# One product of two per-row numbers in the input scale's chain, with two scalar operands instead of a second tensor

## The reference, cut to what matters

```python
def bit_linear(x, w, b):
    gamma_x = clip(max(abs(x), axis=-1), 1e-05, None)
    scale_x = 127.0 / gamma_x
    x_dq = clip(round(x * scale_x), -128.0, 127.0) / scale_x
    gamma_w = clip(mean(abs(w)), 1e-05, None)
    w_dq = clip(round(w / gamma_w), -1.0, 1.0) * gamma_w
    return einsum('bsd,hd->bsh', x_dq, w_dq) + b

x = x + L0_xattn(layernorm(x), ctx)                   # stage A
h = silu(bit_linear(xn, gate_w)) * bit_linear(xn, val_w)   # xn = layernorm(x)
x = x + bit_linear(h, out_w)                          # stage B
x = x + L1_xattn(layernorm(x), ctx)                   # stage D
x = x + L1_ffn(layernorm(x))                          # stage C
```

## Time and profile before

| | us |
|---|---|
| three runs, median | 837.59 |
| lowest and highest of them | 830.35, 840.47 |
| the profiled execution | 840.63 |
| its span, from the first to the last instruction | 838.8 |

### The profile page before, as it was taken

The page is one execution under the profiler, slowest core; times in us unless marked ns, Lnnn a source line. Parts: engine busy times, 40 slices in busy tenths (PEclk is TensorE's granted clock), DMA queues, the critical chain, the costliest instruction groups (busy, mean ns, idle before and its releaser), DMA issues. The chain is left out here.

```text
span 838.8 us, 22126 instructions
## 1 busy us (share of the span) xinstructions
PE 763.0 (91%) x6898; PEld 398.9 (48%) x6898; DVE 752.7 (90%) x1636; ACT 701.4 (84%) x1447; POOL 634.2 (76%) x1139
## 2 busy tenths in 40 slices
PE   2677899999999999999999999999999989898886
PEld 1333444454555554555555555555545445444444
DVE  5688899999899999999999999999989989787865
ACT  3888888888799998999989999999979889688644
POOL 3827566788888887888888888888878877677632
PEclk9557899999999999999999999999999999899989
DMA  9401222244443444454544444544443434344230
GB/s 311 133 21 39 59 75 77 65 114 88 94 115 95 115 97 106 109 112 108 113 109 106 112 110 114 115 99 112 109 97 101 104 84 112 72 91 97 57 69 20
DMA packets 197952, 82.59 MB, mean 98 GB/s; under 512 B 139710, under 2 KB 196670, under 8 KB 197836
## 3 DMA queue, kind: packets, MB, share of 16 engines
q1 hardware_dynamic: 193260, 74.63, 38.1%
q10 hardware_dynamic: 4576, 6.55, 2.4%
HBM read 28.15 MB, written 4.69 MB: 39 GB/s over the span
## 5 line engine op out<-in xcount | busy, mean ns | idle before, releaser
L1120 DVE TENSOR_REDUCE mx<-psS 128x2 f32<-128x512 f32 x512 | 333.3, 679 | 21.0 <-PE psS L617 19.9
L799 ACT ACTIVATE prob<-psT 128x512 f32<-128x512 f32 x512 | 292.4, 603 | 23.2 <-PE psT L625 15.4
L617 PE MATMUL psS<-KQ 31*128 31x256 f16 x1024 | 137.7, 284 | 15.1 <-DVE mx L1120 12.1
L639 PE MATMUL psW<-prob,vst 128*32 128x256 f32 x2048 | 143.0, 400 | 0.0
L728 PE MATMUL psW<-guT,xT 128*128 128x512 bf16 x512 | 133.5, 390 | 6.3 <-DMA xT<-stage 5.1
L625 PE MATMUL psT<-KQ 32*128 32x256 f16 x1024 | 129.4, 280 | 3.9 <-ACT prob L799 3.0
L639 PEld LDWEIGHTS psW<-prob,vst 128*32 128x32 f32 x2048 | 55.2, 112 | 61.5 <-issue 34.6
L728 PEld LDWEIGHTS psW<-guT,xT 128*128 128x128 f16 x512 | 43.3, 99 | 72.8 <-issue 38.8
L1004 POOL TENSOR_TENSOR hqB<-wide,rnd 128x512 bf16<-128x512 f32 x60 | 63.4, 1058 | 14.7 <-ACT wide L847 14.4
L617 PEld LDWEIGHTS psS<-KQ 31*128 31x128 f16 x1024 | 40.0, 93 | 72.4 <-DVE mx L1120 46.1
L1018 POOL TENSOR_TENSOR stage<-stage 128x512 f16<-128x512 f32 x60 | 69.6, 1161 | 2.6 <-ACT stage L908 0.5
(11 more groups left out here) (190 smaller groups left out, 1791.0 us busy)
## 6 DMA issues: line engine op xcount, KB each, us to landing
KQ<-hl SPq DMA_DIRECT2D x192, 64.0 KB, 1.9
xP<-in_x SPq DMA_DIRECT2D x32, 128.0 KB, 2.2
cP<-in_ctx SPq DMA_DIRECT2D x32, 128.0 KB, 2.1
xA<-in_x SPq DMA_DIRECT2D x32, 128.0 KB, 2.6
cB<-in_ctx SPq DMA_DIRECT2D x32, 128.0 KB, 2.3
oV<-uA SPq DMA_DIRECT2D x32, 128.0 KB, 2.1
out<-x SPq DMA_DIRECT2D x32, 128.0 KB, 2.1
oR<-rden_d SPq DMA_DIRECT2D x120, 32.0 KB
```

The lines of the kernel that those rows point to most:

```text
L617: m = nc.tensor.matmul(psS[:, n % 2, T * k:T * k + T], KQ[p % DEEP][r, 1, g, 128 * k:128 * k + 128], KQ[p % DEEP][r, 0, g, :], start=True, ...
L639: m = nc.tensor.matmul(bank[32 * j:32 * j + 32, :], vst[p % DEEP][:, k, 4 * n + j, :], prob[:, (4 * n + j) % 8, k, :], start=(k == 0), sto ...
L799: m = nc.scalar.activation(flat(prob[:, n % 8, :, :]), psT[:, n % 2, :], ACT.Exp, scale=float(HC) ** -0.5)
L1120: m = nc.vector.tensor_reduce(mx[:, p % 2, :, 4 * (n % 4) + n // 4], psS[:, n % 2, :].rearrange("p (c s) -> p c s", c=NK), AX.X, ALU.max)
```

## The change

Line 1195 computes (s * s) * g, with s the scale of a row and g a constant of the weights. Before, the first s is a tensor of 128x1, the second s a per-partition scalar, and g a second tensor, all in SBUF. After, the one tensor is s, and the two scalars are s and g. The operations, their order, the destination and the place in the list are the same.

```diff
@@ -1192,8 +1192,7 @@
                     sc = sB[:, p % 2, :]
                     inner(1, nc.vector.tensor_scalar(sc[:, 1:2], sc[:, 0:1], 1e-5, 1.0 / 127.0, ALU.max, ALU.mult))
                     nc.vector.tensor_scalar(sc[:, 4:5], sc[:, 1:2], gam_q[:, 0:1], None, ALU.mult)
-                    nc.vector.scalar_tensor_tensor(out=sc[:, 5:6], in0=sc[:, 1:2], scalar=sc[:, 1:2],
-                                                   in1=gam_q[:, 1:2], op0=ALU.mult, op1=ALU.mult)
+                    nc.vector.tensor_scalar(sc[:, 5:6], sc[:, 1:2], sc[:, 1:2], gam_q[:, 1:2], ALU.mult, ALU.mult)
                     m = nc.vector.reciprocal(sc[:, 2:3], sc[:, 1:2])
```

## The result

The changed kernel took 827.1 us (median of 20 runs, 822.0 to 837.2) against 834.7 us for the kernel before in the same comparison. The ratio is 0.9924, with a 95% interval from 0.9896 to 0.9951: a gain of 6.3 us, from 4.1 to 8.7, clear of zero and well inside two per cent. The profiled execution's span is 828.4 us; before it was 838.8.

The account below looks back on a forecast made before the run. A loop through VectorE and GpSimd, closed by line 1195's hold, was taken to set the pace. Gains of 6.0 us (steady stretch) and 3.1 us (head and tail), rounded to 9, gave 837.6 - 9 = 828.6 us; range 820 to 838.

Parts of the forecast that it names:

- The hold and its cause: Line 1195 on VectorE, with two SBUF tensors, waits for the running GpSimd instruction: 20.8 us for 32, 13.95 us removable.
- The rival that the new form is held likewise: At line 1195 the new form is held like the old; time stays at 837 to 838 us; chance 0.05.
- The price of the new form: New line 1195: 214 ns each, taken from line 1194, so 6.85 us for 32 instructions.
- The loop: Steady stretch: rot's end releases line 1195, VectorE runs to mvC, which releases GpSimd's rsC; 6.86 + 15.06 = 21.92 us.
- The floor: Shortest interval from pair to pair in the steady stretch; VectorE's period after the change put at 21.29 us.
- GpSimd as next in line: Steady stretch: without rsC's 0.57 us wait for mvC, GpSimd's period is 21.37 us, and GpSimd is late next.
- TensorE as a bound at 21.52 us: Steady stretch: TensorE's busy share, 0.981 x 21.94 us, limits the saving per period to 0.42 us; called a soft bound.
- The sum: Whole kernel: 6.0 us from twelve steady periods plus 3.1 us from head and tail, 9.1, rounded to 9 us.
- the half: Head and tail: of 6.25 us of VectorE's time saved there, half, 3.1 us, reaches the end.
- The slower rival: Late qT transpose landings, priced at 5.2 us each; three more make the kernel 6.6 us slower, 844 us; chance 0.06.
- All of it and more: TensorE's bound is soft and the outlier's loss goes too: 14 to 17 us gained, 821 to 824 us; chance 0.17.
- Another loop at the same pace: A loop among ScalarE, TensorE and VectorE only 0.1 us shorter: 1 to 4 us gained, 834 to 837 us; chance 0.17.

Follow-up runs that it names:

- e2: The changed kernel plus one 128x1 product of two SBUF tensors into a scratch tile behind line 1195; 0.9988 of the kernel before.
- e4: The kernel before with the old two-tensor form of line 1195 moved to just ahead of mvC, where GpSimd waits; 0.9930 of the kernel before.
- e8: The changed kernel with three fillers in the new form (one tensor, two per-partition scalars) ahead of line 1195; 832.8 us, run once only.
- e7: The changed kernel with both products (columns 4 and 5) moved from VectorE to GpSimd, behind rq; 0.9977 of the kernel before, 832.8 us.
- e9: The changed kernel itself, unaltered, compared again with the kernel before on another occasion; 0.9951 of the kernel before.
- e3: The kernel before with three 128x1 one-scalar tensor_scalar fillers ahead of the old line 1195; 1.0057 of the kernel before.
- e5: The changed kernel with the reciprocal 1/s ahead of the two products in the same step; 0.9927 of the kernel before, 830.3 us.
- e6: The kernel before with the old line 1195 placed behind the reciprocal, which keeps the signal; 0.9971 of the kernel before, 833.4 us.

## Why the prediction was right, point by point

**The hold and its cause** were right: 128x1 with two tensors from SBUF waits for GpSimd, with one tensor and two per-partition scalars it does not. e2 and e4 show it from both sides. The rival that the new form is held likewise, for which the earlier trace rows spoke, did not come about at this size (that row is taken up below). SBUF — State Buffer of the Trainium skill, section Who interferes with whom, names both the two-input case and the mode of tensor_scalar; the first agrees with e2 (656 ns in the median against 147), and the second does not show at 128x1 (262 to 268 ns in all 32 executions). At 256 elements it may: the earlier trace rows has two executions of one form, and they differ in what GpSimd does meanwhile.

```profile
806.19 1.24 DVE L1134 TENSOR_SCALAR xnC<-x,mvC,rsC 128x256 f32<-128x256 f32 x1
806.12 2.32 POOL L1018 TENSOR_TENSOR stage<-stage 128x512 f16<-128x512 f32 x2
...
822.77 0.41 DVE L1134 TENSOR_SCALAR xnC<-x,mvC,rsC 128x256 f32<-128x256 f32 x1 [0.71 <-POOL rsC L960]
```

The first begins 0.07 us behind a GpSimd instruction and takes 1.24 us; during the second GpSimd runs nothing. All twelve traces have this pair, 1.23 or 1.24 us and 0.41. So the row spoke rightly for a hold at its own size, and the step from 256 elements to one is what failed of that rival. No run varied the size.

**The price of the new form** was mis-sized: 214 ns taken, 265 measured. The group costs 8.5 us instead of 6.85, so 20.8 - 8.5 = 12.3 us of VectorE's time went, not 13.95. What line 1194 could not show is the second per-partition scalar (e8).

**The loop** was right, and so was its removal. The floor was given as 21.29 us by VectorE's sum; with the true price it is 21.94 - (0.86 - 0.265) = 21.35, and 21.36 to 21.37 was measured. The interval from pair to pair was forecast at 21.3 to 21.5 us; that holds for the floor and not for the mean (21.76 and 21.94).

**GpSimd as next in line** was wrong. I subtracted `rsC`'s 0.57 us and got 21.37 us; but its wait for `mvC` is still there, 6.0 us in 12 periods, even at the shorter pace, where the prediction had it nearly vanish. GpSimd's other small waits were part of the same delay: `hq`'s wait for ScalarE, 0.2 us per pair before, left the list too. So GpSimd's bound lies lower than I put it. e7 shows that it isn't far, as two instructions of 264 and 334 ns used it up.

**TensorE as a bound at 21.52 us** was wrong as a bound: intervals of 21.36 us occur. What replaced it is unevenness. The mean stays 0.4 us above the floor (0.6 in e9), and part of that is transposes that land too late for `Bd` and `bg` (2.3 and 1.3 us in the steady stretch; before, `bg` waited 0.9 us and `Bd` wasn't in the list). Which of the remaining waits is worth how much was not isolated.

**The sum.** For the steady stretch it had 6.0 us; the profiles show 12 x 0.35 = 4.2, and with e9's profile 12 x 0.17 = 2.0. The term was high by the price of the form and by the waits above the floor. For the head and the tail it had 3.1, half of what was held there; the profiles show 10.4 - 4.2 = 6.2 us, and with e9's, whose span is 825.8 us, 11.0. But these differences are not the change's alone: the profiled execution before lies 5.9 us above that kernel's median (840.6 against 834.7), the one after 3.1 us above its own. So the half was not tested, and no run shows it. The total of 9 is 1.5 us above the difference of the medians (7.5), 2.7 above the gain by the ratio (6.3), and 4.9 above that of the second comparison (4.1), which lies below the forecast's 5 to 13 us. That the forecast time of 828.6 us comes within 1.5 us of 827.1 is in part luck: the gain was set too high by 1.5 us or more, and the median that it was taken from was 2.9 us too high.

**The slower rival** did not come about: the `xqT` transpose still lands in 2.4 us in the median. Its price was misread. The interval around 612 us, into which the late landing fell, is long in every trace: 24.8 to 27.9 us between starts of `bsC` in all twelve, 26.89 before and 24.77 after the change, where no `xqT` landed late. By that comparison the landing cost 2.1 us there and not 5.2, and e3 reached its 27.85 us there without a late one. In the steady stretch, intervals with a landing of 3.8 to 4.4 us are 25.20 (e3), 24.25 (e5), 25.23 (e9) and 23.16 us (e7), 1.9 to 3.9 above the floor; such landings occur with the hold (e3) and without it. The rival does have a milder form, landings of `hqT` above 4 us, which takes some of the gain: in the steady stretch there is none in the five kernels with a floor of 21.88 us or more (before, e2, e3, e6, e8), and there are one to four in each profile of the others, three of them in the change's. **All of it and more** is ruled out by the interval, since it needed 14 us and the interval ends at 8.7. **Another loop at the same pace** is ruled out by the floor, though its 1 to 4 us are not far from what the second comparison gave.

## What to carry to other kernels

When a small instruction has a median far above its minimum, look at what another engine is running during it, and compare when it ends, not how long it takes: a constant end with a varying length means that it is released from outside. A hold of this kind does more than take time; it ties one engine's order to another's, and the period of that tie can be read from the interval between repetitions and tested with fillers on either side of the cut. When the tie is gone, expect the floor to fall by the full amount and the mean by less (here 0.58 us, and 0.35 or 0.17 us in two profiles), because other waits, late DMA landings among them, then lie above the floor.

## What the runs showed of the hardware that I had not expected

- A second per-partition scalar makes a 128x1 tensor_scalar on VectorE 0.06 us longer (265 against 204 ns in the same place, and 0.06 us in the floor), and on GpSimd 0.07 us (334 against 264 ns, lines 992 and 991 of e7).
- A 128x1 instruction with two tensors in SBUF that begins shortly before a GpSimd instruction ends can be held for the whole next one: 1.10 us at 455.33 in e3, begun 0.08 us before `rot`'s end, for an instruction that takes 0.21 us alone.
- A tensor_scalar with two per-partition scalars is not held at 128x1 (262 to 268 ns), and at 128x256 it takes 1.24 us while a GpSimd instruction runs and 0.41 us without one (line 1134).
- Whether the reciprocal comes first or last of the three instructions behind the scale makes no difference that the runs could show (0.9927 with the reciprocal first, 0.9924 with it last).
